# Attention values of a key block multiplied for 512 queries at once with every second step, in place of 256 queries with each step

## The chip, the cores and the metric

One core of one Trainium2 chip runs the whole program. The metric is the device time of one execution in microseconds (us); lower is better.

## The reference, cut to what matters

Two layers over 2048 tokens of width 128. The first is a selective scan and a mixture of experts, the second an attention and a sparse mixture of experts. The change is in the attention of the second layer:

```python
def _L1_attn_ref(x, ...):
    D, H, B, L = (128, 16, 2, 256)        # 16 heads of 8; b_ = 1, l_ = 2048 here
    ...
    scores = jnp.einsum('bhqd,bhkd->bhqk', Q, K) / sqrt(DK)
    scores = scores * tau[..., None] + delta[:, :, None, :]
    attn = jax.nn.softmax(scores, axis=-1)
    out = jnp.einsum('bhqk,bhkd->bhqd', attn, V)
    out = out.transpose(0, 2, 1, 3).reshape(b_, l_, D)
    return linear(out, out_w, out_b)
```

## The kernel before, in words

The scan and its experts take the first half of the span. Then comes the attention, and behind it the last experts. The attention works in 16 groups G: four query chunks of 512 tokens by four sets of four heads. A group has 32 steps h. A step takes half of the four heads (two heads, `hh` 0 and 1) of one key block of 128 tokens (`kb = h // 2`). All engines walk through the same function, `attention_order`, and each issues only its own part of a step; every engine works strictly in the order in which it issues. The parts that matter:

- **score** (L963 on TensorE): for each of two heads a matmul of 54 rows by 512 queries in bf16 (L968), one on the upper and one on the lower 64 rows of the array. Results go to the next of three PSUM banks, 0 to 2, in turn. `take_exp(s)` makes the matmul of slot s wait until ScalarE has freed slot s-3.
- **exp** (L1336, L1343 on ScalarE): the exponential of each such bank goes to SBUF, into `Pt[K % 3]`, 128 keys by 4 heads by 512 queries in fp32. `Pt` is part of the buffer that the profile calls `aa`. One signal, `e_free`, tells both that the bank is free and that the exponentials are there.
- **maxima** (L928, L937 on TensorE; L1670 on VectorE): the scores of the next group, computed in advance without their last three rows, for the row maxima. Two matmuls fill a pair of banks (3 and 4, or 5 and 6), and VectorE reduces 2 x 512 elements (`mx`). There is one such unit per step, for the 15 groups after the first; they run 10 units ahead and so end 10 steps before the last group.
- **pv** (L971, L980 on TensorE): the values. `Pt` times the values of the key block, for four heads on the four column groups of the array (32 columns each), summed over the 16 key blocks in bank 7. Each call is an fp32 matmul, which the trace shows as two records. Before the change a unit is 256 of the 512 queries, and a step carries one unit.
- **once a group**: **finish** (L956, the maxima turned, through one slot of the three exp banks), **evac** (L1327, bank 7 to SBUF on ScalarE, behind the exponentials of step 1 of the next group) and **turn** (L985, four transposes L989 at step 3). Groups 4, 8 and 12 also carry **heads** (L997), **project** (L1005 and VectorE L1715, L1397, L1401) and **choose** (VectorE L1727 to L1745). The last group carries five **column** units (L1041).

`next_pv` (L325) sets where pv stands. Its unit lags two to four steps behind the scores: at steps 2 and 3 of a group none is issued, and at steps 12 and 20 two stand in a row. The order within a step is score, maxima, finish if due, pv, then the once-a-group parts.

Of the kernel before, what the change touches and what calls it, by code (L numbers as in the profile page):

```python
# [13 lines left out]
NB = T // 128  # L14
NH = 16
NG = 16
# [217 lines left out]
HALVES = 32  # L234
# [53 lines left out]
def attention_order(p):  # L288

    exps, maxs = Slots(), Slots()  # L290
    maxs.take(FIRST)
    unit = dict(max=AHEAD, expert=0, pv=0)
    done = {}
    p["finish"](0, exps.take())

    def next_max():
        if unit["max"] < (NG - 1) * HALVES:
            G, j = 1 + unit["max"] // HALVES, unit["max"] % HALVES
            unit["max"] += 1
            p["maxima"](G, j, maxs.take())  # L300

    def next_expert():

        u = unit["expert"]
        unit["expert"] += 1
        if u < UNITS:
            p["sorted_up"](u, exps.take())
        if LAG_SORTED <= u < UNITS + LAG_SORTED:
            p["sorted_down"](u - LAG_SORTED)
        if u % 2 and 3 <= u < UNITS - 3:  # L310
            p["pick"]((u + 3) // 2)
        if u == UNITS + LAG_SORTED + 1:
            for b in range(SORTED_TOKENS):
                p["gather"](b)
        i = u - UNITS
        if 0 <= i < 32:
            p["up"](i, exps.take())
        if LAG <= i < 32 + LAG:
            p["down"](i - LAG)
        if i in (18, 22, 26):  # L320
            p["added"]((i - 18) // 4)
        if i == 32 + LAG + 3:
            p["fold"](3, maxs.take())

    def next_pv(G, h):  # L325

        behind = 2 if h < 2 or h >= 20 else 3 if h >= 12 else 4
        while unit["pv"] <= HALVES * G + h - behind:
            last, x = divmod(unit["pv"], HALVES)
            p["pv"](last, x // 2, x % 2, done[unit["pv"] // 2])  # L330
            unit["pv"] += 1

    def after(G, h):

        q, last = G // 4, G % 4 == 3
        if G < 0:
            return
        if h == 1:
            p["evac"](G)
        elif h == 3:  # L340
            p["turn"](G, maxs.take())
        elif last and h == 5:
            p["heads"](q, maxs.take())
        elif last and h == 7:
            p["project"](q, maxs.take())
        elif last and h == 12:
            p["choose"](q)
            if q == 3:
                p["flip"](q, maxs.take())
        elif last and h == 16:  # L350
            if q == 3:
                p["gates"](q, maxs.take())
            elif q == 2:
                p["ranks"](maxs.take())
        elif G == 11 and 18 <= h < 31:
            p["places"]()
        elif G == 12 and h % 2 == 0 and 4 <= h < 28:
            p["scatter"](h // 2 - 2)

    for _ in range(LEAD_MAXIMA - AHEAD):  # L360
        next_max()
    for G in range(NG):
        if G < 4:
            p["weights"](2 * G)
            p["weights"](2 * G + 1)
        if G == 4:
            p["weights"](8)
        for h in range(HALVES):
            t = HALVES * G + h
            p["score"](G, h // 2, h % 2, exps.take(2))  # L370
            done[t // 2] = exps.used
            next_max()
            if unit["max"] % HALVES == 2 and 0 < unit["max"] < (NG - 1) * HALVES:
                p["finish"](unit["max"] // HALVES, exps.take())
            elif t == (NG - 1) * HALVES - LEAD_MAXIMA + 1:
                p["finish"](NG - 1, exps.take())
            next_pv(G, h)
            after(G - 1, h)
            if G == 14 and h in (24, 28):
                p["stage"](h // 4 - 6)  # L380
            elif G == 15 and h % 5 == 4 and h < 25:
                p["column"](h // 5, maxs.take())
                if h < 15:
                    p["stage"](h // 5 + 2)
            elif G == 15 and h == 26:
                p["pick"](0)
    p["pick"](1)
    p["pick"](2)
    for h in range(HALVES):
        if h < 2:  # L390
            next_pv(NG, h)
        after(NG - 1, h)
        next_expert()
    while unit["expert"] < UNITS + 32 + LAG + 4:
        next_expert()


def build(nc, A, out):
    with ExitStack() as ctx:
        S = Signals(nc, ctx)  # L400
# [4 lines left out]
        PS = ctx.enter_context(nc.psum_tensor("PS", [128, 8, 512], F32))  # L405

        def bank(i):
            return PS[:, i, :]
# [28 lines left out]
        va = D[:, 12288:14976].rearrange("p (b c) -> p b c", b=NB)  # L437
# [9 lines left out]
        with ExitStack() as ph:  # L447
            def sa(name, shape, dt=F32):
                return sb(name, shape, dt, ph)
# [51 lines left out]
            G = sa("G", [128, 4, 8])  # L501
            mx = sa("mx", [128, 4, 4])

        with ExitStack() as ph:
# [16 lines left out]
            Pt = [aa[:, 2048 * i:2048 * i + 2048] for i in range(3)]  # L521
# [67 lines left out]
        def freed(m):  # L589

            return S(f"m_free{m % 2}"), m // 2 + 1
# [17 lines left out]
        def tensor_program(e):  # L609
            w = Waits(e)  # L610
# [357 lines left out]
                    e.matmul(take_exp(s + hh), KS[64 * hh:64 * hh + 54, p, 128 * kb:128 * kb + 128],  # L968
                             QP[64 * hh:64 * hh + 54, qc % 2, p, :], start=True, stop=True).then_inc(S("e_full"), 1)

            def pv(G, kb, n, exps):  # L971
                K = 16 * G + kb
                cs = slice(256 * n, 256 * n + 256)
                w.wait_ge(S("e_free"), exps)
                w.wait_ge(S("v"), 16)
                if kb == 0:
                    w.wait_ge(S("Oe"), G)
                for j in range(4):
                    h = 4 * (G % 4) + j
                    t = e.matmul(PS[32 * j:32 * j + 32, 7, cs], va[:, kb, 9 * h:9 * h + 32],  # L980
                                 Pt[K % 3][:, 512 * j + 256 * n:512 * j + 256 * n + 256],
                                 start=(kb == 0 and n == 0), stop=(kb == NB - 1 and n == 1))
                t.then_inc(S("pv"), 1)

            def turn(G, m):  # L985
# [105 lines left out]
            def fold(q, m):  # L1091
                to = take_max(m)
                w.wait_ge(S("x_sum"), 7)
                for b in range(4):
                    t = e.transpose(to[:, 0, 128 * b:128 * b + 128], HA[:, 128 * b:128 * b + 128], ident[:, :])
                t.then_inc(S("m_full"), 1)

            attention_order(ATT_IDLE | dict(maxima=maxima, finish=finish, score=score, pv=pv, turn=turn,
                                            heads=heads, project=project, flip=flip, gates=gates, ranks=ranks,
                                            column=column, sorted_up=sorted_up, sorted_down=sorted_down, up=up,  # L1100
                                            down=down, fold=fold))

        def scalar_program(e):
            w = Waits(e)
# [220 lines left out]
                e.activation(nm, bank(s % 3)[0:4, :], ACT.Copy).then_inc(S("e_free"), 1)  # L1325

            def evac(G):  # L1327
                w.wait_ge(S("pv"), 32 * G + 32)
                if G:
                    w.wait_ge(S("m_full"), slot["turn"] + 1)  # L1330
                e.activation(Oe, bank(7), ACT.Copy).then_inc(S("Oe"), 1)
# [4 lines left out]
            def score(G, kb, n, s):  # L1336
                K = 16 * G + kb
                for hh in range(2):
                    w.wait_ge(S("e_full"), s + hh + 1)
                    if K >= 3:  # L1340
                        w.wait_ge(S("pv"), 2 * (K - 2))
                    c = 512 * (2 * n + hh)
                    e.activation(Pt[K % 3][:, c:c + 512], bank((s + hh) % 3), ACT.Exp).then_inc(S("e_free"), 1)  # L1343

# [787 lines left out]
        def sync_program(e):  # L2132
            w = Waits(e)
# [18 lines left out]
            for x in range(8):  # L2152
                e.dma_start(f_w2[:, 1 + x, :, :], A["L0_ffn_experts_w2"][x].rearrange("(k p) d -> p k d",
                                                                                     p=128)).then_inc(S("d_ffn"), 16)
# [32 lines left out]
            def gates(tc):  # L2187
                yield from idle(4 + 2 * late(tc) - late(tc) // 2)
                w.wait_ge(S("g_row"), tc + 1)
                e.dma_start(gd[tc], gT0[:, :]).then_inc(S("d_gd"), 16)  # L2190
                yield
# [21 lines left out]
            def load_q(qc):  # L2213
                sl = qc % 2
                qs = slice(512 * qc, 512 * qc + 512)
                w.wait_ge(S("d_sq"), 16 * min(qc + 2, 4) if qc else 16)
                w.wait_ge(S("q_ones"), sl + 1)
                if qc >= 2:
                    w.wait_ge(S("pv"), 128 * (qc - 1))
                for hh in range(2):  # L2220
                    for gi, pk in enumerate(grp[0]):
                        e.dma_start(QP[64 * hh + 8 * gi:64 * hh + 8 * gi + 8, sl, :, :],
                                    sc[pk, :, qs].rearrange("(a b r) t -> b r a t", b=2, r=8)[hh]).then_inc(
                            S(f"d_q{sl}"), 16)
# [77 lines left out]
            def gates(q, m):  # L2302
                w.wait_ge(*freed(m))
                e.dma_start(gh, gT[:, :]).then_inc(S("d_gh"), 16)
                w.wait_ge(S("d_gh"), 16)
                w.wait_ge(S("pv"), 32 * NG)
                e.dma_start(HG, gh.partition_broadcast(128)).then_inc(S("d_H"), 16)

            def sorted_down(u):
# [83 lines left out]
```

## Time and profile before

| | |
|---|---|
| median of 3 runs | 1530.22 us (1527.34 to 1535.51) |
| span of the profiled execution | 1529.1 us |
| TensorE busy | 1305.2 us, 85% |
| VectorE busy | 1206.0 us, 79% |
| ScalarE busy | 1058.4 us, 69% |
| GpSimd busy | 668.8 us, 44% |
| mean granted TensorE clock | 0.932 of 2.4 GHz |

The median lies 1.1 us above the span of the profiled execution. Busy shares are means over stages with different limits; for a change in the attention only its own stretch of the trace counts. In the rows PE is the matmuls of TensorE, PEld its weight loads, DVE is VectorE, ACT is ScalarE, POOL is GpSimd.

### The profile page before, as it was taken

The page shows a single profiled execution, that of the slowest core. Times are in us where ns is not written, and L with a number is a line of the kernel's source. Part 1 is how long each engine was busy: PE and PEld are TensorE (multiplying, and loading weights), DVE is VectorE, ACT ScalarE, POOL GpSimd, SP SyncE. Part 2 cuts the span into 40 slices and gives each one's busy share as a digit, 9 for nine tenths or more (in the row PEclk, how much of TensorE's full clock was granted, in tenths as well). Part 3 has the DMA queues.
Part 4 walks back from the last instruction along what each step waited for, and adds up shares of the span by engine and source line. Part 5 has one row for each costly group of instructions (what it writes and reads, how often), then busy time and mean ns, then how long its engine had stood idle before and what let it go on. Part 6 is the DMA issues. An engine that isn't in the chain of part 4 may idle for free.

```text
span 1529.1 us, 22573 instructions
## 1 busy us (share of the span) xinstructions
PE 1305.2 (85%) x8424; PEld 506.3 (33%) x8424; DVE 1206.0 (79%) x1435; ACT 1058.4 (69%) x1839; POOL 668.8 (44%) x652
## 2 busy tenths in 40 slices
PE   4364689988977997886499999999999998999998
PEld 1121234333443443332122222222222222236963
DVE  0799988898989871776699999999999997933522
ACT  3552379768837825453179998999899987997643
POOL 1688868977978856661403112111111123111430
PEclk9677789999988998997689999999999998999999
DMA  8221222223323202421213001100010000010210
GB/s 220 66 82 70 76 66 88 90 70 83 96 70 84 82 21 55 88 43 37 41 35 51 30 30 48 23 2 2 2 23 2 2 2 19 6 29 12 74 32 28
DMA packets 63696, 75.71 MB, mean 50 GB/s; under 512 B 8633, under 2 KB 39226, under 8 KB 63458
## 3 DMA queue, kind: packets, MB, share of 16 engines
q1 hardware_dynamic: 62818, 72.70, 17.9%
q0 software_dynamic: 768, 1.57, 0.3%
q8 instruction: 66, 1.08, 0.3%
q14 instruction: 44, 0.36, 0.1%
HBM read 66.04 MB, written 8.21 MB: 49 GB/s over the span
## 4 chain that ended last, share of the span: by engine, by line
PE 52%; DVE 26%; ACT 9%; issue 7%; POOL 4%; DMA 1%; SPq 1%; another core or an unknown queue 0%; DVEq 0%; POOLq 0%; ACTq 0%
DVE mx L1670 16%; PE PS L980 11%; PE PS L968 6%; PE PS L736 5%; PE PS L745 5%; PE PS L937 4%; PE PS L688 2%; PE PS L1052 2%; PE PS L1067 2%; DVE D L1463 2%; DVE PS L1449 2%; PE PS L1088 2%; PE PS L1076 2%; ACT D L1206 1%; POOL D L1926 1%
## 5 line engine op out<-in xcount | busy, mean ns | idle before, releaser
L1343 ACT ACTIVATE aa<-PS 128x512 f32<-128x512 f32 x1024 | 551.7, 598 | 63.0 <-PE PS L968 51.4
L1670 DVE TENSOR_REDUCE mx<-PS 128x2 f32<-128x1024 f32 x480 | 552.8, 1215 | 15.6 <-PE PS L937 7.3
L980 PE MATMUL PS<-aa,D 128*32 128x256 f32 x4096 | 322.9, 393 | 1.5 <-ACT aa L1343 0.6
L968 PE MATMUL PS<-D 54*128 54x512 bf16 x1024 | 213.1, 391 | 13.0 <-ACT aa L1343 8.3
L2044 POOL CAST n<-nm 4x512 bf16<-4x512 f32 x15 | 9.0, 602 | 453.7 <-ACT nm L1325 453.7
L937 PE MATMUL PS<-D 51*128 51x512 bf16 x960 | 191.3, 386 | 17.2 <-DVE mx L1670 16.6
L1449 DVE TENSOR_TENSOR_SCAN PS<-PS,D 128x512 f32<-128x512 f32 x128 | 157.5, 1231 | 11.1 <-POOL D L1942 3.5
L745 PE MATMUL PS<-xnT,f_w 128*128 128x512 f32 x288 | 158.3, 644 | 6.1 <-ACT HB L1233 5.5
L1233 ACT ACTIVATE HB<-PS 128x512 f32<-128x512 f32 x144 | 84.1, 595 | 104.7 <-PE PS L745 98.4
L736 PE MATMUL PS<-HB,f_w 128*128 128x512 f32 x288 | 146.3, 618 | 6.1 <-DVE GO L1537 5.9
L980 PEld LDWEIGHTS PS<-aa,D 128*32 128x32 f32 x4096 | 84.3, 108 | 192.8 <-issue 154.3
L1206 ACT ACTIVATE D<-D,Am 128x512 f32<-128x512 f32 x128 | 85.1, 713 | 75.7 <-DVE D L1463 73.7
L688 PE MATMUL PS<-D,ident 128*128 128x512 f32 x192 | 107.5, 685 | 32.9 <-POOL D L1933 28.1
L1933 POOL TENSOR_TENSOR D<-D 128x1024 f32<-128x1024 f32 x48 | 112.9, 2353 | 48.5 <-DVE D L1463 48.3
L968 PEld LDWEIGHTS PS<-D 54*128 54x128 bf16 x1024 | 53.4, 93 | 225.3 <-ACT aa L1343 160.1
L1463 DVE TENSOR_TENSOR_SCAN D<-D,hl,PS 128x512 f32<-128x512 f32 x96 | 122.6, 1277 | 2.9
L1926 POOL TENSOR_TENSOR D<-D 128x1024 f32<-128x1024 f32 x48 | 112.8, 2350 | 3.3
L736 PEld LDWEIGHTS PS<-HB,f_w 128*128 128x128 f32 x288 | 57.0, 200 | 82.8 <-issue 70.5
L745 PEld LDWEIGHTS PS<-xnT,f_w 128*128 128x128 f32 x288 | 53.9, 200 | 73.3 <-issue 51.6
L688 PEld LDWEIGHTS PS<-D,ident 128*128 128x128 f32 x192 | 39.4, 213 | 90.6 <-issue 50.9
L1455 DVE SCALAR_TENSOR_TENSOR PS<-PS,D 128x512 f32<-128x512 f32 x96 | 66.8, 696 | 2.8 <-POOL D L1926 0.5
L1942 POOL TENSOR_SCALAR D<-D 128x1024 f32<-128x1024 f32 x64 | 66.5, 1040 | 5.5
(333 smaller groups left out, 1700.2 us busy)
## 6 DMA issues: line engine op xcount, KB each, us to landing
D<-bc SPq DMA_DIRECT2D x128, 256.0 KB, 3.5
GB<-gd SPq DMA_DIRECT2D x32, 256.0 KB, 3.7
D<-sc SPq DMA_DIRECT2D x72, 64.0 KB
aa<-in_L_ffn_W SPq DMA_DIRECT2D x9, 256.0 KB, 3.2
D<-in_L_ffn_W SPq DMA_DIRECT2D x9, 256.0 KB, 3.6
f_w<-in_L_ffn_experts_w SPq DMA_DIRECT2D x1, 2048.0 KB, 9.2
f_w<-in_L_ffn_experts_w SPq DMA_DIRECT2D x8, 256.0 KB, 5.9
aa<-gh SPq DMA_DIRECT2D x1, 2048.0 KB, 8.3
```

Of the source, the lines that this page charges most:

```text
L688: e.matmul(bank(g), ident[:, :], wb[k % 4][:, g, :], start=(n == 0), stop=(n == 15)).then_inc(S("mm_sum"), 1)
L736: e.matmul(down_bank(tc, n // 4), f_w2[:, n // 4, n % 4, :], HB1[i % 6], start=(n % 4 == 0), stop=(n % 4 == 3)).then_inc(S("mm_down"), 1)
L745: e.matmul(bank(4 + i % 2), f_w1[:, n // 4, 128 * (n % 4):128 * (n % 4) + 128], XN[:, ts], start=True, stop=True).then_inc(S("mm_up"), 1)
L937: t = e.matmul(to[:, hh, :], query(hh, qc % 2, p, b), KS[64 * hh:64 * hh + 51, p, 512 * c:512 * c + 512], start=True, stop=True)
L968: e.matmul(take_exp(s + hh), KS[64 * hh:64 * hh + 54, p, 128 * kb:128 * kb + 128], QP[64 * hh:64 * hh + 54, qc % 2, p, :], start=True, sto ...
L980: t = e.matmul(PS[32 * j:32 * j + 32, 7, cs], va[:, kb, 9 * h:9 * h + 32], Pt[K % 3][:, 512 * j + 256 * n:512 * j + 256 * n + 256], start= ...
L1343: e.activation(Pt[K % 3][:, c:c + 512], bank((s + hh) % 3), ACT.Exp).then_inc(S("e_free"), 1)
L1449: e.tensor_tensor_scan(out=bank(3), data0=bank(2), data1=ab[k % 3][:, g, :], initial=0.0, op0=ALU.max, op1=ALU.mult).then_inc(S("sP"), 1)
L1463: e.tensor_tensor_scan(out=pb[k % 2][:, g, :], data0=ab[k % 3][:, g, :], data1=bank(3), initial=hl[:, 16 * g + n:16 * g + n + 1] if tc els ...
L1670: e.tensor_reduce(mx4[:, G % 2, b, 2 * pair:2 * pair + 2, c:c + 1], max_banks(m), AX.X, ALU.max).then_inc(freed(m)[0], 1)
L1926: e.tensor_tensor(wb[k % 4], DU[tc % 2][:, :, :], Bb[k % 3].unsqueeze(1).to_broadcast([128, 2, C]), ALU.mult).then_inc(S("wB"), 1)
L1933: e.tensor_tensor(wb[k % 4], pb[k % 2], Cb[k % 3].unsqueeze(1).to_broadcast([128, 2, C]), ALU.mult).then_inc(S("xC"), 1)
```

## The change

A pv unit now covers all 512 queries of a key block, so there are 16 per group in place of 32. It is issued only at odd steps, three steps behind the first step of its key block (`2 * t + 3 <= 32 * G + h`). The signal `pv` counts 16 a group, and the waits on it are halved accordingly.

```diff
     def next_pv(G, h):
-        behind = 2 if h < 2 or h >= 20 else 3 if h >= 12 else 4
-        while unit["pv"] <= HALVES * G + h - behind:
-            last, x = divmod(unit["pv"], HALVES)
-            p["pv"](last, x // 2, x % 2, done[unit["pv"] // 2])
-            unit["pv"] += 1
+        if h % 2:
+            t = unit["pv"]
+            if 2 * t + 3 <= HALVES * G + h:
+                last, kb = divmod(t, NB)
+                p["pv"](last, kb, done[t])
+                unit["pv"] += 1
...
-            def pv(G, kb, n, exps):
+            def pv(G, kb, exps):
                 K = 16 * G + kb
-                cs = slice(256 * n, 256 * n + 256)
                 w.wait_ge(S("e_free"), exps)
...
-                    t = e.matmul(PS[32 * j:32 * j + 32, 7, cs], va[:, kb, 9 * h:9 * h + 32],
-                                 Pt[K % 3][:, 512 * j + 256 * n:512 * j + 256 * n + 256],
-                                 start=(kb == 0 and n == 0), stop=(kb == NB - 1 and n == 1))
+                    t = e.matmul(PS[32 * j:32 * j + 32, 7, :], va[:, kb, 9 * h:9 * h + 32],
+                                 Pt[K % 3][:, 512 * j:512 * j + 512], start=(kb == 0), stop=(kb == NB - 1))
                 t.then_inc(S("pv"), 1)
...
             def evac(G):
-                w.wait_ge(S("pv"), 32 * G + 32)
+                w.wait_ge(S("pv"), 16 * G + 16)
...
                     if K >= 3:
-                        w.wait_ge(S("pv"), 2 * (K - 2))
+                        w.wait_ge(S("pv"), K - 2)
```

TensorE's order around step 3 of a group (the rows L989 or L988 are its turn; L968 or L969 the scores, L937 or L938 the maxima, L980 the values). Before:

```order
L968 MATMUL PS<-D 128x512 x2
L937 MATMUL PS<-D 128x512 x2
L980 MATMUL PS<-aa,D 32x256 x4
L968 MATMUL PS<-D 128x512 x2
L937 MATMUL PS<-D 128x512 x2
L968 MATMUL PS<-D 128x512 x2
L937 MATMUL PS<-D 128x512 x2
L989 MATMUL PS<-ident,aa 128x128 x4
L968 MATMUL PS<-D 128x512 x2
L937 MATMUL PS<-D 128x512 x2
L980 MATMUL PS<-aa,D 32x256 x4
```

After:

```order
L969 MATMUL PS<-D 128x512 x2
L938 MATMUL PS<-D 128x512 x2
L980 MATMUL PS<-aa,D 32x512 x4
L969 MATMUL PS<-D 128x512 x2
L938 MATMUL PS<-D 128x512 x2
L969 MATMUL PS<-D 128x512 x2
L938 MATMUL PS<-D 128x512 x2
L980 MATMUL PS<-aa,D 32x512 x4
L988 MATMUL PS<-ident,aa 128x128 x4
L969 MATMUL PS<-D 128x512 x2
L938 MATMUL PS<-D 128x512 x2
```

Before, values stood behind nearly every pair of score and maxima; the pair without them, at steps 2 and 3, occurred once a group. Now two steps follow each other without values between them everywhere, and then a values unit of twice the columns comes.

TensorE's order at the end of the last group, where there are no maxima (L1052 or L1051 belongs to the experts behind). Before:

```order
L968 MATMUL PS<-D 128x512 x2
L980 MATMUL PS<-aa,D 32x256 x4
L968 MATMUL PS<-D 128x512 x2
L980 MATMUL PS<-aa,D 32x256 x8
L1052 MATMUL PS<-xnT,own0 128x128 x4
```

After:

```order
L969 MATMUL PS<-D 128x512 x4
L980 MATMUL PS<-aa,D 32x512 x4
L969 MATMUL PS<-D 128x512 x4
L980 MATMUL PS<-aa,D 32x512 x4
L1051 MATMUL PS<-xnT,own0 128x128 x4
```

Four score matmuls now stand in a row, for three exp banks.

## Rows read from the trace of the kernel before

**Rows 1.** Page: granted clock of TensorE in 40 slices of the span, in tenths.
```profile
PEclk9677789999988998997689999999999998999999
```

**Rows 2.** Busy time by stretch: inner groups, then the last group.
```profile
core 0: us, PE busy (x) PEld busy (x) DVE busy (x) ACT busy (x) POOL busy (x), PEclk, DMA share, GB/s
808.00:963.00 155.00, 149.56 (x1584) 41.23 (x1580) 152.25 (x157) 141.99 (x265) 30.19 (x106) 1.00 0.17 39
1359.00:1396.00 37.00, 35.51 (x351) 12.48 (x343) 4.58 (x8) 33.64 (x67) 0.01 (x1) 1.00 0.12 35
```

**Rows 3.** Timeline, a step with maxima (start, us, engine, line, operation).
```profile
1010.25 0.64 PE L980 MATMUL PS<-aa,D 128*32 128x256 f32 x8
...
1010.83 0.39 PE L968 MATMUL PS<-D 54*128 54x512 bf16 x2
...
1011.05 0.38 PE L937 MATMUL PS<-D 51*128 51x512 bf16 x2
1011.37 0.64 PE L980 MATMUL PS<-aa,D 128*32 128x256 f32 x8
1011.93 0.10 PEld L968 LDWEIGHTS PS<-D 54*128 54x128 bf16 x2 [0.41 <-ACT aa L1343]
```

**Rows 4.** Timeline, VectorE reductions in the same stretch.
```profile
1009.31 3.48 DVE L1670 TENSOR_REDUCE mx<-PS 128x2 f32<-128x1024 f32 x3
```

**Rows 5.** Timeline, step 12 of a group: two values units in a row.
```profile
1015.80 1.07 PE L980 MATMUL PS<-aa,D 128*32 128x256 f32 x16
...
1016.81 0.39 PE L968 MATMUL PS<-D 54*128 54x512 bf16 x2
```

**Rows 6.** Timeline, steps 2 and 3 of a group: no values between scores.
```profile
1003.25 0.39 PE L968 MATMUL PS<-D 54*128 54x512 bf16 x2
...
1003.48 0.38 PE L937 MATMUL PS<-D 51*128 51x512 bf16 x2
1003.53 0.60 ACT L1331 ACTIVATE aa<-PS 128x512 f32<-128x512 f32 x1
...
1003.70 0.39 PE L968 MATMUL PS<-D 54*128 54x512 bf16 x1
...
1004.68 0.09 PEld L968 LDWEIGHTS PS<-D 54*128 54x128 bf16 x1 [0.89 <-ACT aa L1343]
...
1004.69 0.60 PE L937 MATMUL PS<-D 51*128 51x512 bf16 x2
...
1005.98 0.39 PE L968 MATMUL PS<-D 54*128 54x512 bf16 x2
```

**Rows 7.** Timeline: the first exponential of rows 6 alone, and two together.
```profile
1004.01 0.62 ACT L1343 ACTIVATE aa<-PS 128x512 f32<-128x512 f32 x1
...
1006.40 1.08 ACT L1343 ACTIVATE aa<-PS 128x512 f32<-128x512 f32 x2 [0.31 <-PE PS L968]
```

**Rows 8.** Scores line: records, duration min/median/max, first and last start.
```profile
L968 PE MATMUL PS<-D x1024: 386/387/631, 769.4 to 1394.8; 54*128 54x512 bf16 x171
```

**Rows 9.** Timeline: turns in groups 4, 5, 7; last a finish, from the chain.
```profile
925.77 0.55 PE L989 MATMUL PS<-ident,aa 128*128 128x128 f32 x3
...
967.58 0.66 PE L989 MATMUL PS<-ident,aa 128*128 128x128 f32 x4
...
1043.21 0.55 PE L989 MATMUL PS<-ident,aa 128*128 128x128 f32 x3
...
1028.94 0.53 PE PS L960 x4
```

**Rows 10.** Timeline, VectorE's wait in group 13.
```profile
1283.94 1.23 DVE L1670 TENSOR_REDUCE mx<-PS 128x2 f32<-128x1024 f32 x1 [3.77 <-remote]
```

**Rows 11.** Timeline, a step at the half clock, start of the attention.
```profile
775.74 0.61 PE L968 MATMUL PS<-D 54*128 54x512 bf16 x2
...
776.71 1.08 PE L980 MATMUL PS<-aa,D 128*32 128x256 f32 x8
777.72 0.39 PE L968 MATMUL PS<-D 54*128 54x512 bf16 x2
```

More of the change, by code:

```diff
@@ L2218, in load_q @@
                 if qc >= 2:
-                    w.wait_ge(S("pv"), 128 * (qc - 1))
+                    w.wait_ge(S("pv"), 64 * (qc - 1))
                 for hh in range(2):
@@ L2305, in gates @@
                 w.wait_ge(S("d_gh"), 16)
-                w.wait_ge(S("pv"), 32 * NG)
+                w.wait_ge(S("pv"), 16 * NG)
                 e.dma_start(HG, gh.partition_broadcast(128)).then_inc(S("d_H"), 16)
```

## The prediction

> **What bounds the kernel now.** I first read the granted clock by slices [rows 1]: it is full from about slice 21 on, which covers nearly the whole attention, so no term below needs a slower clock except at the start. Then busy time by stretch [rows 2]. In the inner groups TensorE shows 149.6, VectorE 152.3 and ScalarE 142.0 of 155 us: three engines near their limit, so shares alone do not tell which of them sets the pace. In the last group, without maxima, VectorE falls to 4.6 of 37 us and ScalarE, with 33.6, remains close to the limit. The timeline of one step tells more. TensorE repeats scores, maxima, values in 10.83 to 11.94 = 1.11 us [rows 3]: 0.22 from scores to maxima, 0.32 from maxima to values, 0.57 from values to the next scores. VectorE's three reductions last 3.48 us, of which the last one counts whole (1.22), so they follow each other every 1.13 us [rows 4]. VectorE is therefore the pace in the long run, and TensorE at 1.11 merely catches up after the once-a-group parts. An ordinary group takes (1043.21 - 967.58) / 2 = 37.8 us [rows 9], of which 32 x 1.13 = 36.2 are reductions. The whole attention, from the first score to the last, takes 1394.8 - 769.4 = 625.4 us [rows 8].
>
> Third, ScalarE's role. The weight load of the next scores ends a wait on the exponential of the last ones (PEld L968 <-ACT, in rows 3), although the values in between hid nearly all of it. So the round trip from scores to exponential to free bank is about as long as a step. That is the number on which this change hangs.
>
> **What the change takes away.** A values unit of 256 queries takes 0.57 us up to the next scores; two in a row take 16.81 - 15.80 = 1.01 [rows 3, 5]. The second costs only 0.43, so about 0.14 of each visit is the price of coming and going, and another 0.1 lies ahead of it (0.32 after the maxima in place of the 0.22 after the scores). One visit for two steps in place of two saves about 0.25 us a pair of steps, on TensorE alone. Neither VectorE's nor ScalarE's work shrinks by a single instruction. A unit of 512 queries streams the same columns as the two in a row, hence 1.0 us. The Trainium skill, TensorEngine Tiling (Array Packing), section Key Properties, says that a change of tiling mode drains the array. By that rule alone the change is a gain, and that outcome is priced as the first rival.
>
> **What the change adds.** Two steps now follow each other without values between them. There are three exp banks and each step fills two, so the second score of the odd step needs the bank of the even step's first score, and TensorE stands still until ScalarE has freed it. The trace has this case once a group [rows 6]: scores at 1003.25, maxima 1003.48, first score of the next step 1003.70, the second only at 1004.68. The maxima behind it, whose banks were free, also waited, until 1004.69. In that place an evacuation held ScalarE up first (L1331). Without it the wait is shorter, and I build it from its parts: a score takes 0.39 [rows 8]; ScalarE starts 0.03 to 0.04 later (5.98 + 0.39 to 6.40) [rows 6, 7]; one exponential takes 0.60 to 0.62, and the bank is taken 0.05 after its end (4.63 to 4.68) [rows 6, 7]. Sum: the second odd score starts 1.08 us after the even scores.
>
> From there: its maxima start with it, on the other half of the array, and the second one 0.22 later (0.60 for the two in place of 0.38 [rows 6]); values follow 0.32 after that; values take 1.0 up to the next scores. **A pair of steps on TensorE: 1.08 + 0.22 + 0.32 + 1.00 = 2.62 us** (I take 2.615), against 2 x 1.13 = 2.26 at VectorE's pace. Is another engine slower than that? ScalarE needs 4 x 0.49 = 1.96 (two exponentials in 1.08 us, so one each 0.49) [rows 7], and VectorE 2.26, so both go idle and TensorE's chain with ScalarE's round trip becomes the pace. In the old order the same round trip of 1.08 lay beside 0.57 us of values and the switches; that cover is what is gone. The buffers of exponentials cause no wait: the first exponential of key block K needs the values of K-3, issued three steps before.
>
> The parts of the sum, first score to last score:
> - 15 groups of 16 pairs at 2.615: 627.6 us.
> - In these, 15 finishes at 0.53 and 14 turns at about 0.69 (the 0.60 for four transposes, with 0.09 for the switch, estimated from 0.32 against 0.22 in rows 3) [rows 9]. All stand behind an odd step's maxima, where nothing covers them: 17.6 us.
> - The last group has no maxima, so its pair is 0.22 shorter, 2.39: 15 pairs, and 1.08 for the last one, 36.9. Its turn 0.69, and of five column units the two at odd steps, 1.4 (the other three fall into the new gap): 39.0 us.
> - Heads, project and choose lengthen a group by 967.58 - 925.77 - 37.8 = 4.0 us now [rows 9]. What TensorE does of that stays, and VectorE's share is partly taken up by its new idle time of 0.35 a pair: between 2.4 and 4.0, I take 3.2, three times: 9.6 us.
> - Group 13 loses some 8.7 us around indirect transfers, one wait of 3.77 in it [rows 10]. I keep it: 8.7 us. The new gaps could hide up to all of it, so the range goes down by that much.
>
> Together 702.5 us against 625.4: 77 us more. Before the attention nothing changes, and the experts behind it start from the same state, later. On the profiled execution 1529.1 + 77.1 = 1606.2, and the median stands 1.1 above its span: **1607 us**, slower by 5.0%.
>
> **Bounds of this.** The round trip from its parts is uncertain by about 0.05, over 250 pairs 12 us either way. Group parts give +2.4 and -2.4, group 13 down to -8.7. Own range: 1588 to 1622.
>
> **Rivals.**
> - *Faster, the switches are the pace.* If the second odd score did not wait, TensorE would need 1.96 a pair and VectorE's 2.26 would hold. A group would be 32 x 1.13 + 0.6 for the turn on VectorE and some 0.3 of group ends, 37.1 against 37.8; 15 groups give 11 us. The last group would go at ScalarE's 1.96 a pair against some 2.1, 2 us. Time: 1530 - 13 = 1517. It decides if the round trip is under 0.7 us. For it speaks the price of switches; against it the standstill in rows 6, and that an exponential alone takes 0.60. Chance 3%.
> - *No change, VectorE covers it.* If TensorE ran so far ahead that the wait fell into VectorE's time, the pair stays at 2.26 and the time at 1530. It decides if round trip and rest come under 2.26 a pair, which means 0.36 us less than the parts above add up to. Two pairs of maxima banks cannot give that lead, as the maxima stand behind the waiting score. Chance 4%.
> - *Much slower, the clock falls too.* TensorE now streams for four times 0.22 and 0.85 of 2.62 us and stands still in each pair. At the half clock [rows 11] scores and maxima are about twice as far apart and values take 1.01 for 256 queries. There, the pair would be some 1.3 + 0.43 + 0.5 + 1.9 = 4.1 us. A tenth of 700 us at that clock costs 70 x (1 - 2.62 / 4.1) = 25 us: about 1632. Against it: the last group of the kernel before, with only scores and values, kept the clock at 1.00 [rows 2]. Chance 5%.
> - *Half as slow.* ScalarE's round trip is partly covered, because TensorE gets past the waiting score with the loads or maxima behind it. Then the maxima (0.22) and part of the switch fall out of the pair: 2.35 to 2.5, time 1545 to 1580. Against it: in rows 6 the maxima did not get past. Chance 6%.
> - That the change does not do what it says is excluded by the order of instructions: it shows the units of 512 columns behind every second step.
>
> **How the numbers follow.** The forecast has 82%. Its own range of 1588 to 1622 leaves a few per cent of it on either side; the range given is 1585 to 1626 and leaves out the faster and the equal case, most of the half-slow one and of the fallen clock, and little else, about 2 in 10. A measurement of this kernel can tell about 0.5%, 8 us, from no change. Faster by more: 3%. Within it: 4%. Slower by more: 93%.
>
> **What would show it.** In the profile after: two steps as score, maxima, score, a gap of about 0.2 to 0.3 us with no matmul, second score 1.08 after the first pair, then 1.0 us of values; 2.6 us from pair to pair; ordinary groups 43.1 us apart; waits of scores for ScalarE's exponentials once in each pair that nothing covers; VectorE down from 98% to about 86% and ScalarE from 92% to some 80% in an inner group; first to last score near 702 us. The prediction is wrong if VectorE stays at 98% there, if the second odd score starts with the first, or if groups lie 37 to 38 us apart.

## The result and the profile after

| | before | after |
|---|---|---|
| median | 1532.55 us (1527.34 to 1535.51, 4 runs) | 1609.47 us (1607.78 to 1609.87, 4 runs) |
| span of the profiled execution | 1529.1 us | 1606.0 us |
| ratio after / before | | 1.0507 (95% interval 1.049 to 1.0523) |

A fourth run of the kernel before moves its median from 1530.22 to 1532.55. Slower by 5.1%, where 5.0% was forecast. The time lies in the attention: first to last score took 625.4 us [rows 8] and now takes 1472.1 - 768.8 = 703.3. These rows answer to [rows 2] and [rows 8]. The view by line of the changed kernel:

```profile
L969 PE MATMUL PS<-D x1024: 376/386/631, 768.8 to 1472.1; 54*128 54x512 bf16 x171
```

Busy time by stretch, the inner groups and then a part of the last group (columns as in [rows 2]):

```profile
808.00:978.00 170.00, 152.32 (x1040) 33.91 (x1036) 152.76 (x153) 132.20 (x258) 29.70 (x104) 1.00 0.16 35
...
1434.00:1472.00 38.00, 31.94 (x203) 8.84 (x203) 4.58 (x8) 31.65 (x63) 0.00 (x0) 1.00 0.07 20
```

In the inner groups all three engines now have room: TensorE 90%, VectorE 90%, ScalarE 78% of the stretch, against 96, 98 and 92% in [rows 2]. In the last group TensorE and ScalarE fall to 84 and 83%. All three became less busy at once, so the work of no single engine can be the bound; the rows below show that a chain through two of them is. The clock was 1.00 in both stretches. A pair of steps in the timeline of the changed kernel:

```profile
1051.14 0.39 PE L969 MATMUL PS<-D 54*128 54x512 bf16 x2
...
1051.37 0.38 PE L938 MATMUL PS<-D 51*128 51x512 bf16 x2
...
1051.57 2.07 ACT L1342 ACTIVATE aa<-PS 128x512 f32<-128x512 f32 x4 [0.54 <-PE PS L969]
1051.59 0.38 PE L969 MATMUL PS<-D 54*128 54x512 bf16 x1
1051.79 2.36 DVE L1669 TENSOR_REDUCE mx<-PS 128x2 f32<-128x1024 f32 x2 [0.25 <-PE PS L938]
...
1052.22 0.39 PE L969 MATMUL PS<-D 54*128 54x512 bf16 x1 [0.25 <-ACT aa L1342]
1052.22 0.60 PE L938 MATMUL PS<-D 51*128 51x512 bf16 x2
...
1052.75 1.07 PE L980 MATMUL PS<-aa,D 128*32 128x512 f32 x8
...
1053.75 0.39 PE L969 MATMUL PS<-D 54*128 54x512 bf16 x2
```

The second odd score starts at 1052.22, 1.08 us after the even scores at 1051.14, released by ScalarE. Its maxima start with it, values at 1052.75, next scores at 1053.75: 2.61 us. In the same 2.61 us ScalarE is idle 0.54 and VectorE 0.25. The chain of waits (each piece is what the next one waited for) shows the loop of the changed kernel in one piece; before the change that view had no ScalarE in an ordinary group:

```profile
1052.82 1.00 PE PS L980 x8
1053.82 0.37 PE PS L969 x2
1054.18 0.59 ACT aa L1342
1054.78 0.05 issue
1054.83 0.39 PE PS L969
1055.21 0.22 PE PS L938 x2
```

Over the whole span ScalarE rose from 9% to 15% of the chain and VectorE fell from 26% to 14%; the scores' wait for ScalarE's exponentials rose from 8.3 to 71.9 us. From the pages before and after: the chain by engine, and the scores' line with what ended its waits:

```profile
PE 52%; DVE 26%; ACT 9%; issue 7%; POOL 4%; DMA 1%; SPq 1%; another core or an unknown queue 0%; DVEq 0%; POOLq 0%; ACTq 0%
...
L968 PE MATMUL PS<-D 54*128 54x512 bf16 x1024 | 213.1, 391 | 13.0 <-ACT aa L1343 8.3
...
PE 56%; ACT 15%; DVE 14%; issue 8%; POOL 5%; DMA 1%; SPq 1%; another core or an unknown queue 0%; DVEq 0%; POOLq 0%; ACTq 0%
...
L969 PE MATMUL PS<-D 54*128 54x512 bf16 x1024 | 294.1, 389 | 72.6 <-ACT aa L1342 71.9
```

The turns of TensorE, one per group, answer to [rows 9]. First a group with heads, project and choose (948.24 to 994.49), then an ordinary one (1037.52 to 1080.55):

```profile
948.24 0.65 PE L988 MATMUL PS<-ident,aa 128*128 128x128 f32 x4
...
994.49 0.66 PE L988 MATMUL PS<-ident,aa 128*128 128x128 f32 x4
...
1037.52 0.66 PE L988 MATMUL PS<-ident,aa 128*128 128x128 f32 x4
...
1080.55 0.66 PE L988 MATMUL PS<-ident,aa 128*128 128x128 f32 x4
```

An ordinary group takes 43.03 us in place of 37.8, the other 46.25 in place of 41.8.

### The profile page after: what moved, and what is told of

It reads as the page before. It is cut to its first block, busy times and chain, and to the rows that moved or that the text cites. A ratio compares the mean times of both kernels' runs of the same rounds, so it can differ in the third digit from the quotient of the medians.

```text
span 1606.0 us, 18462 instructions
## 1 busy us (share of the span) xinstructions
PE 1331.2 (83%) x6376; PEld 477.5 (30%) x6376; DVE 1220.4 (76%) x1435; ACT 1036.9 (65%) x1839; POOL 668.7 (42%) x652
## 4 chain that ended last, share of the span: by engine, by line
PE 56%; ACT 15%; DVE 14%; issue 8%; POOL 5%; DMA 1%; SPq 1%; another core or an unknown queue 0%; DVEq 0%; POOLq 0%; ACTq 0%
PE PS L980 15%; PE PS L969 11%; ACT aa L1342 9%; PE PS L737 5%; PE PS L746 4%; PE PS L938 3%; DVE D L1462 3%; DVE PS L1448 3%; PE PS L1051 2%; PE PS L1066 2%; PE PS L689 2%; DVE PS L1454 2%; PE PS L1087 2%; PE PS L1075 2%; POOL D L1925 2%
## 5 line engine op out<-in xcount | busy, mean ns | idle before, releaser
L1342 ACT ACTIVATE aa<-PS 128x512 f32<-128x512 f32 x1024 | 528.7, 604 | 158.8 <-PE PS L969 154.1
L1669 DVE TENSOR_REDUCE mx<-PS 128x2 f32<-128x1024 f32 x480 | 567.0, 1221 | 62.5 <-PE PS L938 59.7
L969 PE MATMUL PS<-D 54*128 54x512 bf16 x1024 | 294.1, 389 | 72.6 <-ACT aa L1342 71.9
L980 PE MATMUL PS<-aa,D 128*32 128x512 f32 x2048 | 276.3, 612 | 0.0
L938 PE MATMUL PS<-D 51*128 51x512 bf16 x960 | 238.2, 389 | 13.0 <-DVE mx L1669 12.0
L969 PEld LDWEIGHTS PS<-D 54*128 54x128 bf16 x1024 | 72.7, 94 | 427.3 <-ACT aa L1342 358.4
L980 PEld LDWEIGHTS PS<-aa,D 128*32 128x32 f32 x2048 | 40.6, 108 | 102.0 <-issue 101.9
```

The costliest lines, as they stand in the source:

```text
L938: t = e.matmul(to[:, hh, :], query(hh, qc % 2, p, b), KS[64 * hh:64 * hh + 51, p, 512 * c:512 * c + 512], start=True, stop=True)
L980: t = e.matmul(PS[32 * j:32 * j + 32, 7, :], va[:, kb, 9 * h:9 * h + 32], Pt[K % 3][:, 512 * j:512 * j + 512], start=(kb == 0), stop=(kb = ...
L1669: e.tensor_reduce(mx4[:, G % 2, b, 2 * pair:2 * pair + 2, c:c + 1], max_banks(m), AX.X, ALU.max).then_inc(freed(m)[0], 1)
```

## The experiments

Each was timed beside the kernel before on the same chip. One chip gave 1523.9 us for the kernel before, another 1530.8, so ratios are compared and not times. An expected time such as 1565 meant a ratio of 1565 / 1532.5.

### Order alone: units of before, both at the odd step

```diff
-        behind = 2 if h < 2 or h >= 20 else 3 if h >= 12 else 4
-        while unit["pv"] <= HALVES * G + h - behind:
+        while h % 2 and unit["pv"] // 2 * 2 + 3 <= HALVES * G + h:
```

> The order of the change with the units of before: values stay in units of 256 queries, but both units of a key block are issued one after the other at the odd step. Theory (the exposed round trip of the exponential): two units in a row take 1.01 us as one of 512 does, the second odd score still starts 1.08 after the even scores, a pair of steps takes 2.62 us, ordinary groups 43.1 us, time 1609 us within 5. Rival A (the width of 512 columns is what costs): the time goes back to 1533. Rival B (both count half): about 1570.

Measured: 1601.33 us against 1523.9, ratio 1.0507 (1.047 to 1.0543), the very ratio of the change. The timeline of this kernel, whose values are two units of 256:

```profile
1050.18 0.39 PE L967 MATMUL PS<-D 54*128 54x512 bf16 x2
...
1051.26 0.39 PE L967 MATMUL PS<-D 54*128 54x512 bf16 x1 [0.25 <-ACT aa L1342]
...
1051.79 1.07 PE L979 MATMUL PS<-aa,D 128*32 128x256 f32 x16
1052.80 0.39 PE L967 MATMUL PS<-D 54*128 54x512 bf16 x2
```

Again 1.08 to the second odd score and 1.01 for the values. The order has the whole effect, within the noise of the runs; the width of the unit is worth the difference of 1.01 and 1.00 in a pair. Rival A falls, and so does rival B.

### Maxima of odd steps ahead of the scores

In `attention_order` of the changed kernel:

```diff
+            if h % 2:
+                next_max()
             p["score"](G, h // 2, h % 2, exps.take(2))
             done[t // 2] = exps.used
-            next_max()
+            if not h % 2:
+                next_max()
```

> The changed kernel, with the maxima of odd steps ahead of the scores in place of behind them. TensorE has the same work in the same number of visits. Theory: the maxima fill the gap, so behind the second odd score (1.08 after the even ones) only the switch (0.31) and the values (1.00) remain: a pair takes 2.39 us in place of 2.61, ordinary groups 39.6 us in place of 43.0, time about 1565 us (1555 to 1575). Rival (TensorE's own work or its switches set the pace): no change, 1609.

Measured: 1558.29 us, ratio 1.023 (1.0197 to 1.0263). Against the change that is 2.6% of its time back, though every engine issues the same instructions as in the changed kernel. The timeline of this kernel:

```profile
1050.31 0.39 PE L972 MATMUL PS<-D 54*128 54x512 bf16 x2
...
1050.54 0.84 PE L941 MATMUL PS<-D 51*128 51x512 bf16 x4
...
1051.70 1.07 PE L983 MATMUL PS<-aa,D 128*32 128x512 f32 x8
1052.70 0.39 PE L972 MATMUL PS<-D 54*128 54x512 bf16 x2
```

All four maxima now stand in the gap, and the pair takes 52.70 - 50.31 = 2.39 us as expected. The same TensorE work in the same number of visits takes less time, so its work was not the pace.

### Changed kernel with exponentials of half the queries

```diff
+                    m = 512 if K < 19 else 256
-                    e.activation(Pt[K % 3][:, c:c + 512], bank((s + hh) % 3), ACT.Exp).then_inc(S("e_free"), 1)
+                    e.activation(Pt[K % 3][:, c:c + m], bank((s + hh) % 3)[:, 0:m], ACT.Exp, scale=0.0 if 16 <= K < 19 else 1.0).then_inc(S("e_free"), 1)
```

> The changed kernel with exponentials of only 256 of the 512 queries from the fourth key block of the second group on; the other half of the buffer keeps ones, so half of the attention is left out of the computation. TensorE and VectorE have the same work as in the changed kernel. Theory: an exponential lasts some 0.38 us in place of 0.60 and the exposed round trip shrinks by that: pair about 2.40 us, group about 39.6, time 1560 us (1550 to 1570), although ScalarE was idle a fifth of the time. Rival (TensorE's work, or the width of the values, sets the pace): 1609.

Measured: 1552.83 us, ratio 1.0196 (1.0161 to 1.0231). The round trip in its timeline:

```profile
1051.39 0.39 PE L969 MATMUL PS<-D 54*128 54x512 bf16 x2
...
1051.81 1.24 ACT L1343 ACTIVATE aa<-PS 128x256 f32<-128x256 f32 x4 [1.15 <-PE PS L969]
...
1052.25 0.09 PEld L969 LDWEIGHTS PS<-D 54*128 54x128 bf16 x1 [0.53 <-ACT aa L1343]
```

From the scores to the weight load of the second odd score 0.86 in place of 1.08. An engine that had been idle for a fifth of the time was given less work, and the kernel lost 3% of its time: what counts here is how long one exponential lasts, not how busy ScalarE is.

### Control: the same edit in the kernel before

> Control: the kernel of before with exponentials of only 256 of the 512 queries from the fourth key block of the second group on; the rest keeps ones, so half of the attention is left out of the computation. Theory: there the round trip is covered by values in each step and VectorE sets the pace, so a shorter exponential brings little: some 0.1 us per ordinary group and 4 to 5 us in the last group, which has no maxima; time 1526 us (1522 to 1530). Rival (ScalarE or its round trip sets the pace in the kernel of before as well): 0.2 us a step, 1430 to 1450.

Measured: 1523.11 us against 1530.82, ratio 0.9953 (0.9938 to 0.9968). Turns of ordinary groups in its timeline:

```profile
1007.10 0.44 PE L989 MATMUL PS<-ident,aa 128*128 128x128 f32 x2 [0.48 <-DVE mx L1671]
...
1044.84 0.44 PE L989 MATMUL PS<-ident,aa 128*128 128x128 f32 x2 [0.48 <-DVE mx L1671]
```

37.74 us in place of 37.81. The same 0.2 us off each exponential that is worth 3.0% in the changed kernel is worth 0.5% here, most of it outside the ordinary groups, in which it is 0.07 us: between the first and the last score 7.3 us are gone, and the last group, without maxima, has 4.1 of them. In the kernel before the exponential lay beside the values; the change took that cover away.

### Half of VectorE's reductions, in the changed kernel and in the one before

The same two edits in both kernels, each line cut here to its arguments:

```diff
-                e.tensor_reduce(mx4[...], max_banks(m), AX.X, ALU.max)
+                e.tensor_reduce(mx4[...], max_banks(m)[:, :, 0:256], AX.X, ALU.max)
...
-                    e.activation(Pt[K % 3][:, c:c + 512], bank((s + hh) % 3), ACT.Exp)
+                    e.activation(Pt[K % 3][:, c:c + 512], bank((s + hh) % 3), ACT.Exp, scale=0.25)
```

> The changed kernel with VectorE's reductions of the advance maxima over 256 of each 512 columns: VectorE has about half of its work, TensorE and ScalarE have all of theirs. The maxima of half of the keys are left out, and the exponentials are taken of a quarter of the scores so that nothing overflows. Theory: VectorE was idle in the changed kernel because it waited for TensorE's chain, so halving its work changes nothing in an ordinary group (43.0 us); only the three groups with heads, project and choose lose 1 to 2 us each. Ratio to before 1.047 (1.043 to 1.051). Rival (VectorE still counts, through its banks): groups under 42 us, ratio under 1.03.

> The kernel of before with the same edit: reductions of the advance maxima over 256 of each 512 columns, exponentials of a quarter of the scores, so the maxima of half of the keys are left out. Theory: VectorE's 1.13 us a step was the pace, and right behind it stand TensorE's work and the round trip with 1.11: ordinary groups go from 37.8 to 37.3 us, the groups with heads and so on lose 2.4 us, ratio to before 0.989 (0.985 to 0.993). Rival (VectorE alone bounds before, the next limit is far): groups of 30 us, ratio 0.93. Rival (VectorE is no bound of before): 1.00.

Measured: ratio 1.0463 (1.0437 to 1.0489) for the changed kernel and 0.9899 (0.9875 to 0.9923) for the one before, which ran 1508.4 us against 1523.32. Turns of ordinary groups, changed kernel:

```profile
1038.19 0.44 PE L988 MATMUL PS<-ident,aa 128*128 128x128 f32 x2
...
1081.24 0.44 PE L988 MATMUL PS<-ident,aa 128*128 128x128 f32 x2
```

and kernel before:

```profile
1000.98 0.44 PE L989 MATMUL PS<-ident,aa 128*128 128x128 f32 x2
...
1038.26 0.44 PE L989 MATMUL PS<-ident,aa 128*128 128x128 f32 x2
```

43.05 us: VectorE's work is worth nothing in an ordinary group of the changed kernel; the 0.4% by which the ratio fell lies elsewhere. 37.28 in place of 37.81: in the kernel before VectorE's work was worth half a microsecond a group. The next limit, 1.11 a step on TensorE, stood right behind it, as the chain of waits of this last kernel shows:

```profile
1008.34 0.32 PE PS L968 x2
...
1009.45 0.32 PE PS L968 x2
```

In the kernel before, the same view changes hands inside a group:

```profile
999.68 6.88 DVE mx L1670 x6
...
1006.61 0.39 PE PS L937 x2
...
1030.62 2.36 DVE mx L1670 x2
```

From 1006.6 to 1030.6, 24 of the 37.8 us of a group, TensorE's own 1.11 a step was the pace, and VectorE's reductions for nearly all of the rest. So neither bounded that kernel alone, and there was little room on TensorE for a loss. That a loss of a few hundredths of a microsecond a step would show at once follows from this by argument; no run tests a loss so small.

### Kernel before with half of the values

```diff
-                cs = slice(256 * n, 256 * n + 256)
+                cs = slice(256 * n, 256 * n + 128)
...
-                                 Pt[K % 3][:, 512 * j + 256 * n:512 * j + 256 * n + 256],
+                                 Pt[K % 3][:, 512 * j + 256 * n:512 * j + 256 * n + 128],
```

> The kernel of before with values units of 128 columns in place of 256: half of the queries' values are left out. Theory: VectorE (1.13 us a step) is the pace of before, and even the round trip of 1.08 is behind it, so 0.21 us less of TensorE's work a step brings only the group ends: groups 37.0 us, last group 2.5 us shorter, time 1518 us (1513 to 1524). Rival (TensorE sets the pace of before): 0.2 us a step, 1430 to 1440.

Measured: 1540.43 us, ratio 1.0064 (1.0042 to 1.0086). Half of the values' columns is gone and the kernel is slower. Both theories missed. Busy time by stretch of this kernel, the inner groups and the last group, with the granted clock behind POOL's column:

```profile
808.00:963.00 155.00, 144.69 (x1558) 51.36 (x1558) 150.12 (x155) 136.69 (x262) 30.25 (x106) 0.93 0.17 38
...
1366.00:1404.00 38.00, 36.48 (x341) 13.86 (x341) 4.57 (x8) 32.83 (x66) 0.00 (x0) 0.78 0.12 34
```

The clock was 1.00 in both in [rows 2]. Here it drops to 1.2 GHz again and again; from 1045.2 to 1048.5, for one, the granted clock is 0.50. Its turns tell a group at the full clock from one in which it falls:

```profile
1008.02 0.44 PE L989 MATMUL PS<-ident,aa 128*128 128x128 f32 x2 [0.70 <-DVE mx L1670]
...
1045.05 0.63 PE L989 MATMUL PS<-ident,aa 128*128 128x128 f32 x2 [0.70 <-DVE mx L1670]
1083.01 0.47 PE L989 MATMUL PS<-ident,aa 128*128 128x128 f32 x1 [0.70 <-DVE mx L1670]
```

The first of these groups takes 37.03 us, which is the 37.0 of the theory; the next, in which the clock falls, 37.96. In the chain of waits of the first (1008 to 1045) VectorE's reductions have 98.3%. So at the full clock 0.21 us less of values a step was worth 0.8 us a group and not 6.7: VectorE stood right behind TensorE too. But with half of the values' columns gone TensorE's clock fell, and over the whole kernel that cost more than the values saved. What else the clock depends on was not tested.

### Values always two steps behind (three in the last group), in the kernel before

```diff
-        behind = 2 if h < 2 or h >= 20 else 3 if h >= 12 else 4
+        behind = 2 if h < 2 or G < NG - 1 else 3
```

> The kernel of before, with values always two steps behind (three in the last group), in place of two to four: no step of a group is without values, none has two units. Theory: the round trip is then covered in each step, also at steps 2 and 3 of a group, and the group is nearer to VectorE's 32 x 1.13: ordinary groups 37.2 us in place of 37.8, last group 1 us shorter, time about 10 us under that of before: 1522. Rival (VectorE hides these places anyway): no change that can be told, 1532.

Measured: 1513.97 us against 1523.9, ratio 0.9938 (0.9913 to 0.9964), or 9.4 us. Its turns:

```profile
1000.86 0.44 PE L989 MATMUL PS<-ident,aa 128*128 128x128 f32 x2
...
1037.99 0.44 PE L989 MATMUL PS<-ident,aa 128*128 128x128 f32 x2
```

37.13 us a group, where 37.2 was expected. This is the cover theory turned into a gain: the kernel before had one bare pair of steps per group [rows 6], and with values behind each step the 0.7 us that it cost are gone; over 15 groups that is 15 x 0.68 = 10 us, about what was measured. The chain of waits of this group has no reduction in it: what is left is TensorE's 1.11 a step, and not VectorE's pace as the theory had it. It is the fastest of all versions that compute the whole attention, ahead of both the kernel before and the change.

## Why the prediction was right, point by point

- **The pair of steps.** 1.08 + 0.22 + 0.32 + 1.00 = 2.62, taken as 2.615, was forecast; 2.61 was measured, with the second odd score 1.08 after the even ones. That the round trip binds and not TensorE's work is shown by three runs: the order alone has the whole effect, the odd step's maxima put into the gap give half of it back, and a shorter exponential shortens the pair.
- **What the change takes away.** The saving in switches is real: a unit of 512 takes 1.00, two in a row 1.01, two apart 2 x 0.57 [rows 3, 5]. It did not reach the span, since the wait that the new order exposes is larger: without it TensorE would need 1.96 us a pair (the first rival's figure), with it the pair is 2.61. The rule of the Trainium skill, TensorEngine Tiling (Array Packing), Key Properties, that a change of tiling mode drains the array, fits these prices, though no run changes the mode alone.
- **The kernel before.** "VectorE is therefore the pace in the long run, and TensorE at 1.11 merely catches up" is half of it: while TensorE catches up, 24 of 37.8 us, the chain of waits is TensorE's. The forecast did not hang on this, as both stand at 1.11 to 1.13 a step.
- **Group parts.** Ordinary groups 43.03 us against 43.1. The first group with heads and so on took 3.2 us longer than an ordinary one (46.25 - 43.03), as taken; the third, next to the stall, took 4.6 longer (1346.59 - 1298.93 from turn to turn).
- **The last group.** 1472.1 - 1433.2 = 38.9 us from its first score to its last against 39.0:

```profile
1433.23 0.39 PE L969 MATMUL PS<-D 54*128 54x512 bf16 x2
```

- **Group 13.** 8.7 us was kept as it stood. The rows after show it again. The turns behind groups 12 and 13 are 49.94 us apart:

```profile
1346.59 0.66 PE L988 MATMUL PS<-ident,aa 128*128 128x128 f32 x4
...
1396.53 0.66 PE L988 MATMUL PS<-ident,aa 128*128 128x128 f32 x4
```

  So it cost 6.9 us in group 13 this time. VectorE waited 3.06 us for a result of the turn, released by something that the view does not name (`remote`):

```profile
1351.04 0.26 DVE L1705 RECIPROCAL rs<-PS 128x16 f32<-128x16 f32 x1 [3.06 <-remote]
```

  Behind it, from 1350.6 to 1360.8, the granted clock was 0.50, the one place after the start of the attention where it fell; the kernel before shows the same from 1282.9 to 1293.0. This agreement is partly luck. The profiled execution of the order-alone kernel, with the same 43.1 us groups, has no such stall, and its first to last score took 697.3 us. The stall comes in some executions and not in others, whatever the order. The term belonged in the range, and only with a chance in the sum.
- **The sum.** 702.5 forecast, 703.3 measured; 1607 forecast, 1609.5 measured. Its parts are less exact than that, and that they cancel is luck. Without the stall the sum is 693.8, and the order-alone kernel, which had none, took 697.3. The stall was smaller than taken, and the first group, which starts at the half clock, took 813.7 - 768.8, about 45 us, nearly 2 more than an ordinary one; the sum has no term for that (the second group's first score starts at 813.7).
- **The rivals.** No faster case, since the round trip is 1.08 where under 0.7 was needed. VectorE did not cover it. The clock did not fall in the changed kernel but for the 10 us behind the stall. The half-values run shows that the clock can fall in this attention when TensorE has less to do, so this rival was no empty one. Nor did TensorE get past the waiting score: the maxima start with it.
- **What the profile would show.** VectorE "about 86%" was said for an inner group; the pair alone gives 2.36 of 2.61, or 90%. Its last reduction's record runs 0.1 past its pace of 1.13, so busy time counts more than 2 x 1.13. The reading was off, not the mechanism.

## What to carry to other kernels

Before you group work on an in-order engine, list what each piece of it covered where it stood. Here a values unit of 0.57 us in each step, with scores and maxima, covered a round trip of 1.08 through ScalarE; with every second cover gone, each pair of steps cost 0.35 us more, though TensorE had less to do. With three buffers and two used per step, as here, the next step waits for the time from fill to free unless other work lies beside it, so spread that work evenly, and put what can stand in a gap ahead of the waiting instruction. And if all engines get less busy while the time grows, look for the loop between them in the chain of waits.

## What was not expected of the hardware

- Less work for TensorE cost time. With values units of half the columns its clock fell to 0.93 on average in the inner groups and 0.78 in the last, against 1.00 with whole units, and the kernel was 0.6% slower. The changed kernel, though TensorE stands still for about 0.25 us in each 2.61, kept 1.00 in its inner groups and in the last.
- A stall in group 13, of 7 to 9 us, beside indirect transfers that GpSimd issues, was in four of the ten profiled executions (before, after, and the two controls with half exponentials and half values in the kernel before) and absent in the others, though they issue the same transfers. Its cause stays open; it was not tested. It may be part of the spread of 8 us between the runs of the kernel before.
